# Moving SyncE's row tiles in layer one of a three-layer graph kernel

## The chip, the cores and the metric

The kernel runs on one core of a Trainium2 chip. The metric is the device time of one execution, in microseconds (us). The chip has five engines in a core that matter here: TensorE (PE in the profile, PEld for its weight loads), VectorE (DVE), ScalarE (ACT), GpSimd (POOL) and SyncE (SP), which only issues transfers.

## The reference

A graph of 6,250 nodes with 128 features each and 106,250 directed edges, sorted by their end node, each edge of one of eight types. Three layers follow one another, then a residual and a normalization of each row:

```
def layer(x, src, dst, edge_type, W, W_root, b):
    out = x @ W_root + b
    x_src = x[src]
    for r in range(8):
        mask = (edge_type == r)
        agg = segment_sum(x_src * mask, dst)
        cnt = segment_sum(mask, dst)
        out += (agg / maximum(cnt, 1)) @ W[r]
    return out
h = x
for i in range(3):
    h = layer(h, ...);  if i < 2: h = relu(h)
return layernorm(x + h)
```

## The kernel before

The edges are cut into 832 tiles of 128 edges, four tiles to a slot (`GT`), 208 slots (`NQ`) a layer. For each tile the rows `x[src]` of its 128 edges are brought from the node table in HBM to one place of `ring`, an SBUF buffer of 26 slots (`G`). Slot q lies at place q % 26 of the ring, so its tiles can only be loaded once slot q - 26 has been used.

Three engines load tiles, each in its own way:

- GpSimd loads most of them (`gather`, L432): one indirect transfer of 128 rows for each tile, L439, in order of slots. Before each slot it takes a credit `ring_free`. The instruction itself keeps GpSimd busy for about 0.94 us.
- SyncE loads 14 tiles a layer (`gather_rows`, L346), the last tile of 14 chosen slots. It reads the row numbers into registers and issues 128 transfers of one row each (L369), one tile after the other. From slot 26 on it takes a credit `sync_slot_free` ahead of a tile.
- ScalarE loads 8 tiles a layer in the same manner (`gather_rows`, L864, issued at L878), at slots 26, 50, ... 194, in pieces of 8 rows between its other work.

`owners` (L68) says which tile is whose; GpSimd leaves out what is in the list. `OWNERS[0]` is layer one's list, `OWNERS[1]` that of layers two and three: `kind` is 0 in layer one alone. Before, the two lists are equal: SyncE has slots 20, 34, 48, ... 202, 14 apart.

Each slot then passes through three engines. VectorE writes the one-hot matrices of its four tiles (`weigh`, L646). TensorE (`sum_edges`, L1135) waits for the slot's gathers, then for SyncE's or ScalarE's rows if it has such a tile, and sums the rows of each tile by node and type (L1153). ScalarE (`evacuate`, L890) gives back the slot (`ring_free`, and `sync_slot_free` if the slot 26 further on has a tile of SyncE) and copies the sums out of PSUM (L902), one copy a slot. After each second slot TensorE multiplies them by the eight weight matrices (`apply_types`, L1157), and VectorE adds the result to `out_t`.

In layer one the same three engines also look up the weight 1/count of each edge, 13 slots ahead (`turn`, `look_up`, VectorE's `cells`), so this layer has more work for each slot, up to slot 195. Ahead of it lies the setup: edges are turned to columns, counts are made, `x` is transposed. GpSimd starts to gather as soon as the source numbers are ready (`src_cols_ready`), during the setup, and SyncE too.

Between two layers TensorE turns `out_t` to rows, ScalarE and VectorE apply the relu, SyncE writes them to `node_table` in HBM, and only then gives GpSimd `table_ready`; the next layer's first gather waits for it.

Of the kernel before, what the change touches and what calls it, by code (L numbers as in the profile page):

```python
# [25 lines left out]
GT = 4  # L26
G = 26
# [8 lines left out]
NQ = NT // GT  # L36
FREES = G // 2
LOADS = 8
SYNC_TILES = 14
# [24 lines left out]
def spread(first, last, n):  # L64
    return [first + (last - first) * k // max(n - 1, 1) for k in range(n)]


def owners(kind):  # L68

    sync = {q * GT + GT - 1: "sync" for q in spread(20, NQ - 6, SYNC_TILES)}  # L70
    act = {q * GT + GT - 2: "act" for q in range(G, NQ - 8, SPACE)}
    return {**sync, **act}


OWNERS = [owners(kind) for kind in range(2)]
BPAD = BUCKETS + BWIN

# [1162 lines left out]
```

## Time and profile before

| | |
|---|---|
| median of 3 runs | 3231.51 us (3230.74 to 3236.58) |
| the profiled execution | 3242.82 us, its span 3241.0 us |
| mean granted clock of TensorE | 0.787 of full speed |
| GpSimd (POOL) busy | 2309.5 us, 71% |
| TensorE (PE) busy | 2111.5 us, 65% |
| VectorE (DVE) busy | 1251.7 us, 39% |
| ScalarE (ACT) busy | 553.7 us, 17% |

The times of the table and of all rows are microseconds from the start of the span. A share of busy time is a mean over setup, three layers and the passages between them, which differ in what they wait for; the rows below are therefore taken from single stretches. Issuing a transfer doesn't count as busy for ScalarE and SyncE, but the rows of a timeline show when transfers are issued and for how long a run of them lasts.

### The profile page before, as it was taken

To read this page: it belongs to the slowest core of one execution; us is meant where nothing else is said; L and a number is where in the kernel's file an instruction comes from. 1 tells how busy PE (TensorE), PEld (TensorE's weight loads), DVE (VectorE), ACT (ScalarE), POOL (GpSimd) and SP (SyncE) were. 2 spreads that over 40 slices of the span, in tenths; PEclk is the share of its full clock that TensorE was granted. 3 is DMA by queue.
4 is the path that set the end of the run, shared out by engine and by line. 5 is a ranking of instruction groups with operands and counts; after the bars stand their busy time and mean duration, and the time that the engine had idled before them with its cause. 6 is when DMAs were issued, how large, how long until landed. Compare 5 with 4: busy or idle time off the path is not lost. (4 is left out here: it accounts for less than half of the span.)

```text
span 3241.0 us, 78756 instructions
## 1 busy us (share of the span) xinstructions
PE 2111.5 (65%) x13004; PEld 1936.7 (60%) x13004; DVE 1251.7 (39%) x5754; ACT 553.7 (17%) x983; POOL 2309.5 (71%) x2445
## 2 busy tenths in 40 slices
PE   7977777777667566566666556556656556656656
PEld 6866666666556445555556556555555555556556
DVE  5544444444434433333333333333333333333334
ACT  1122222222222221111111111112111111111113
POOL 6657777777777177777777777747777777777773
PEclk9978888888878877777767776768777877777777
DMA  3112222222222122222222222232222222222232
GB/s 103 46 37 56 56 56 56 56 56 56 55 56 56 53 61 56 55 55 56 56 56 55 56 56 55 56 82 55 56 55 55 56 56 56 56 55 56 55 94 63
DMA packets 124472, 187.87 MB, mean 58 GB/s; under 512 B 48603, under 2 KB 82026, under 8 KB 123978
## 3 DMA queue, kind: packets, MB, share of 16 engines
q0 software_dynamic: 77760, 159.41, 18.8%
q1 hardware_dynamic: 40026, 21.85, 2.4%
q14 instruction: 375, 3.07, 0.3%
q8 instruction: 119, 1.95, 0.2%
q10 hardware_dynamic: 6192, 1.60, 0.2%
HBM read 173.06 MB, written 9.60 MB: 56 GB/s over the span
## 5 line engine op out<-in xcount | busy, mean ns | idle before, releaser
L439 POOL DMA_INDIRECT ring<-node_table,src_t x1620 | 1532.8, 946 | 586.6 <-issue 433.3
L1153 PE MATMUL ps_a<-onehot,ring 128*128 128x128 f32 x4992 | 897.0, 335 | 980.0 <-DMA ring<-node_table,src_t 755.9
L649 DVE TENSOR_SCALAR onehot<-iota,key,weight 128x128 f32<-128x128 f32 x2496 | 885.9, 368 | 1424.7 <-DVEq L266 1415.2
L1153 PEld LDWEIGHTS ps_a<-onehot,ring 128*128 128x128 f32 x4992 | 771.0, 236 | 1055.9 <-DMA ring<-node_table,src_t 710.9
L439 POOL DMA_INDIRECT ring<-in_x,src_t x810 | 774.3, 956 | 296.2 <-issue 190.1
L1163 PE MATMUL ps_o<-sums,w_rel 128*128 128x128 f32 x4992 | 937.7, 367 | 62.4 <-PEq L266 62.3
L1163 PEld LDWEIGHTS ps_o<-sums,w_rel 128*128 128x128 f32 x4992 | 917.8, 284 | 71.8 <-issue 71.8
L902 ACT COPY sums<-ps_a 128x512 f32<-128x512 f32 x624 | 364.8, 585 | 2331.4 <-ACTq L266 2174.5
L660 DVE TENSOR_TENSOR out_t<-out_t,ps_o 128x16 f32 x2496 | 437.4, 175 | 51.2 <-DVEq L266 36.4
L531 DVE TENSOR_TENSOR oh_cell<-cell_t,iota_bf 128x256 bf16<-128x256 bf16 x208 | 61.2, 295 | 407.7 <-DVEq L266 372.6
L888 ACT CAST oh_cell_t<-ps_r 64x512 bf16<-64x512 f32 x202 | 116.9, 579 | 139.9 <-ACTq L266 139.5
L1099 PE MATMUL ps_r<-ident_bf,oh_cell 128*64 128x128 bf16 x808 | 95.1, 244 | 3.1 <-PEq L266 3.0
L1099 PEld LDWEIGHTS ps_r<-ident_bf,oh_cell 128*64 128x64 bf16 x808 | 65.8, 146 | 29.0 <-issue 7.9
L1116 PE MATMUL ps_w<-inv_parts,oh_cell_t 64*128 x832 | 63.0, 169 | 14.4 <-PEq L266 13.5
L1116 PEld LDWEIGHTS ps_w<-inv_parts,oh_cell_t 64*128 64x128 bf16 x832 | 41.5, 94 | 35.6 <-issue 20.7
L1053 PE MATMUL ps_r<-h_t,w_root 128*128 128x512 f32 (+1 forms) x78 | 43.4, 682 | 27.1 <-PEq L266 25.8
L1062 PEld LDWEIGHTS ps_a<-count_bkt,count_cell 128*64 128x64 bf16 x416 | 50.9, 216 | 5.3 <-issue 5.3
L1062 PE MATMUL ps_a<-count_bkt,count_cell 128*64 128x32 bf16 x416 | 52.4, 292 | 1.1 <-PEq L266 1.1
L1062 PE MATMUL ps_o<-count_bkt,count_cell 128*64 128x32 bf16 x416 | 52.1, 291 | 0.0
L1062 PEld LDWEIGHTS ps_o<-count_bkt,count_cell 128*64 128x64 bf16 x416 | 51.2, 217 | 0.0
L1053 PEld LDWEIGHTS ps_r<-h_t,w_root 128*128 128x128 f32 x78 | 14.2, 216 | 56.2 <-issue 56.0
L578 DVE TENSOR_TENSOR count_cell<-cell_t,iota_bf 128x1024 bf16<-128x1024 bf16 x52 | 35.7, 686 | 0.0
(140 smaller groups left out, 418.0 us busy)
## 6 DMA issues: line engine op xcount, KB each, us to landing
ring<-node_table SPq DMA_DIRECT2D x3584, 0.5 KB
ring<-node_table ACTq DMA_DIRECT2D x2048, 0.5 KB
ring<-in_x SPq DMA_DIRECT2D x1792, 0.5 KB
ring<-node_table,src_t POOLq DMA_INDIRECT x1620
ring<-in_x ACTq DMA_DIRECT2D x1024, 0.5 KB
ring<-in_x,src_t POOLq DMA_INDIRECT x810
node_table<-ring SPq DMA_DIRECT2D x24, 256.0 KB
out_rows<-ring SPq DMA_DIRECT2D x12, 256.0 KB
```

What stands on the lines that cost most here:

```text
L439: nc.gpsimd.indirect_dma_start(out=ring[:, q % G, t, :], out_offset=None, in_=source, in_offset=bass.IndirectOffsetOnAxis(ap=src_t[:, q * ...
L531: nc.vector.tensor_tensor(oh_cell[:, b, :, :], cell_t[:, q * GT:(q + 1) * GT].unsqueeze(1).broadcast_to([P, CELLS, GT]), iota_bf[:, :, 0:G ...
L649: ins = nc.vector.tensor_scalar(onehot[:, b, t, :], iota_1[:, :], key[:, col:col + 1], weight[:, col:col + 1], ALU.is_equal, ALU.mult)
L660: nc.vector.tensor_tensor(here, here, ps_o[b][:, at:at + WIN], ALU.add).then_inc(added, 1)
L888: nc.scalar.copy(oh_cell_t[:, b, :], bank[0:CELLS, :]).then_inc(turned_full[b], 1)
L902: nc.scalar.copy(sums[:, b, :, at:at + GT, :].rearrange("p r t w -> p t r w"), ps_a[a][:, :].rearrange("p (t r w) -> p t r w", r=R, t=GT))\
L1053: nc.tensor.matmul(ps_r[b][:, 0:block_cols(n)], w_root[:, :], h_t[:, n * BLK:n * BLK + block_cols(n)], start=True, stop=True).then_inc(r_f ...
L1062: ins = nc.tensor.matmul(ps_c[h][0:CELLS, 0:BWIN], count_cell[:, h, :, t], count_bkt[:, h, :, t], start=(t == 0), stop=(t == CT - 1))
L1099: ins = nc.tensor.matmul(bank[0:CELLS, t * P:(t + 1) * P], oh_cell[:, b, :, t], ident_bf[:, :], start=True, stop=True)
L1116: ins = nc.tensor.matmul(ps_w[r][:, at:at + NEAR * PARTS], oh_cell_t[:, b, t * P:(t + 1) * P], inv_parts[:, bass.ds(bucket[t], NEAR), :].r ...
L1153: ins = nc.tensor.matmul(ps_a[b][:, t * KEYS:(t + 1) * KEYS], ring[:, q % G, t, :], onehot[:, b, t, :], start=True, stop=True)
L1163: ins = nc.tensor.matmul(ps_o[b][:, 0:PAIR * WIN], w_rel[:, r, :], sums[:, b, r, :, :].rearrange("p t w -> p (t w)"), start=(r == 0), stop ...
```

## The change

In layer one SyncE's 14 tiles belong to the slots 14, 24, 28, 43, 58, 74, 89, 105, 120, 136, 151, 167, 182 and 198, instead of 20, 34, 48, 62, 76, 90, 104, 118, 132, 146, 160, 174, 188 and 202. The number stays 14. The tiles of slots 20, 34, ... in layer one pass to GpSimd, those of the new slots from GpSimd to SyncE. ScalarE's tiles and layers two and three are as they were.

```
 def owners(kind):

-    sync = {q * GT + GT - 1: "sync" for q in spread(20, NQ - 6, SYNC_TILES)}
+    at = spread(20, NQ - 6, SYNC_TILES) if kind else [14, 24] + spread(G + 2, NQ - 10, SYNC_TILES - 2)
+    sync = {q * GT + GT - 1: "sync" for q in at}
     act = {q * GT + GT - 2: "act" for q in range(G, NQ - 8, SPACE)}
     return {**sync, **act}
```

## Rows read from the trace of the kernel before

**Rows 1.** The page's busy times: engine, busy us, share of the span, instructions.
```profile
PE 2111.5 (65%) x13004; PEld 1936.7 (60%) x13004; DVE 1251.7 (39%) x5754; ACT 553.7 (17%) x983; POOL 2309.5 (71%) x2445
```

**Rows 2.** Timeline of POOL: start, length, what; in brackets the idle time before.
```profile
149.06 1.37 POOL L439 DMA_INDIRECT ring<-in_x,src_t  x1 [0.30 <-issue]
188.00 0.94 POOL L439 DMA_INDIRECT ring<-in_x,src_t  x1 [37.57 <-POOLq L266]
...
1072.62 0.94 POOL L439 DMA_INDIRECT ring<-in_x,src_t  x1 [0.30 <-issue]
1137.64 0.94 POOL L439 DMA_INDIRECT ring<-node_table,src_t  x1 [64.08 <-issue]
...
2149.86 0.94 POOL L439 DMA_INDIRECT ring<-node_table,src_t  x1 [0.30 <-issue]
2179.58 0.94 POOL L439 DMA_INDIRECT ring<-node_table,src_t  x1 [28.77 <-POOLq L266]
```

**Rows 3.** Windows of L439 alone: stretch, length, POOL busy (gathers), TensorE's clock, DMA.
```profile
188.00:1074.00 886.00, 670.13 (x707) 0.84 0.21 56
1137.00:2151.00 1014.00, 766.32 (x810) 0.74 0.21 56
```

**Rows 4.** Timeline of SyncE's queue.
```profile
28.37 66.15 SPq L369 DMA_DIRECT2D ring<-in_x  x128
...
219.12 65.91 SPq L369 DMA_DIRECT2D ring<-in_x  x128
...
896.04 66.01 SPq L369 DMA_DIRECT2D ring<-in_x  x128
...
963.63 133.70 SPq L369 DMA_DIRECT2D ring<-in_x  x256
```

**Rows 5.** Who waited for L369's rows, in all layers; timeline of PE.
```profile
  PE ps_a L1153: 66.2, 7
...
692.94 2.08 PE L1153 MATMUL ps_a<-onehot,ring 128*128 128x128 f32 x8 [4.51 <-DMA ring<-in_x]
...
1098.43 2.08 PE L1153 MATMUL ps_a<-onehot,ring 128*128 128x128 f32 x8 [18.66 <-DMA ring<-in_x]
```

**Rows 6.** Windows of ScalarE's copies L902 alone, one copy a slot.
```profile
298.00:691.50 393.50, 53.69 (x92) 0.86 0.22 56
762.00:824.00 62.00, 7.73 (x14) 0.78 0.22 56
```

**Rows 7.** Timeline of ACT, L902: slots 2, 3, 26, 117, 194, 201, 203, 207; layer two's 207.
```profile
191.84 0.58 ACT L902 COPY sums<-ps_a 128x512 f32<-128x512 f32 x1 [2.28 <-ACTq L266]
...
199.93 0.58 ACT L902 COPY sums<-ps_a 128x512 f32<-128x512 f32 x1 [3.91 <-ACTq L266]
...
298.24 0.58 ACT L902 COPY sums<-ps_a 128x512 f32<-128x512 f32 x1 [1.64 <-ACTq L266]
...
691.06 0.58 ACT L902 COPY sums<-ps_a 128x512 f32<-128x512 f32 x1 [3.62 <-ACTq L266]
...
1058.93 0.58 ACT L902 COPY sums<-ps_a 128x512 f32<-128x512 f32 x1 [1.68 <-ACTq L266]
...
1080.04 0.59 ACT L902 COPY sums<-ps_a 128x512 f32<-128x512 f32 x1 [2.07 <-ACTq L266]
...
1104.44 0.58 ACT L902 COPY sums<-ps_a 128x512 f32<-128x512 f32 x1 [2.99 <-ACTq L266]
...
1114.85 0.58 ACT L902 COPY sums<-ps_a 128x512 f32<-128x512 f32 x1 [2.01 <-ACTq L266]
...
2155.69 0.58 ACT L902 COPY sums<-ps_a 128x512 f32<-128x512 f32 x1 [5.30 <-ACTq L266]
```

**Rows 8.** Windows of all engines: PE, PEld, DVE, ACT, POOL busy; clock; DMA.
```profile
298.20:416.40 118.20, 89.22 (x693) 80.69 (x692) 58.85 (x280) 30.44 (x56) 89.51 (x95) 0.88 0.22 56
...
751.70:1058.90 307.20, 206.40 (x1518) 186.12 (x1519) 133.74 (x634) 68.14 (x127) 232.13 (x247) 0.81 0.21 56
...
96.00:162.00 66.00, 64.92 (x424) 53.57 (x423) 36.99 (x75) 10.90 (x18) 41.63 (x43) 1.00 0.17 45
```

## The prediction

> **What bounds the kernel now.** I read the busy shares first, then GpSimd's gathers one by one, then what every other engine waits for in layer one. GpSimd is busy 71% of the span, more than any other engine [rows 1], and its gathers (POOL, L439) start every 1.25 us with 0.30 us between them: it is never free while a layer's gathers run. In layer one 707 gathers start between 188.00 and 1072.62, 884.62 / 706 = 1.253 us apart; layer two has 810 in one unbroken run [rows 2, 3]. Once its gathers have begun it stands still only three times: from 150.4 to 188.0, when it has filled the 26 slots of the ring and no slot has been given back; for 64.1 us between layers one and two (start to start 65.02); and for 28.8 us between two and three (29.72) [rows 2]. The same work lies between two layers both times, so 35.3 us of the first gap want a reason.
>
> The reason is SyncE. It loads its row tiles by 128 single-row transfers in 66 us, and starts one tile every 67.6 us (896.04 to 963.63) when nothing holds it [rows 4]. Its first tile (slot 20) is issued from 28.4 to 94.5; then it stands idle until 219.12, because the second tile belongs to slot 34 and slot 8 must have been used first. From there it never rests: 13 tiles end at 1097.33 (the row of 256 starts at 963.63 and takes 133.70) [rows 4], 24 us after GpSimd's last gather. TensorE waits 66.2 us for these rows in 7 waits, the first at slot 118 (4.51 us) and the last, 18.66 us, at slot 202, whose matmuls start at 1098.43, 1.1 us after the last transfer was issued [rows 5].
>
> Why it falls behind: with no wait for SyncE, the chain of TensorE, ScalarE and VectorE takes (691.06 - 298.24) / 91 = 4.317 us a slot from slot 26 to slot 117 (ScalarE's copies L902, one a slot; 92 lie in that stretch) [rows 6, 7]. 14 slots are 60.4 us against SyncE's 67.6, so each tile loses 7.2 us. The tile of slot 34 is in at 286, needed at 298.24 + 8 x 4.317 = 332.8: 46.7 us early. After 6.5 tiles that is used up, at slot 118 to 132, where the waits begin. In layer one TensorE trails GpSimd by a whole ring at first, as it starts late; in layer two it is close behind at the end: the last copy at 2155.69, the last gather at 2149.86 [rows 2, 7]. Layer one's last copy is at 1114.85, 42.2 us behind.
>
> **The change, part by part.** (1) Slots 14 and 24 both lie in the first filling of the ring, so neither waits for a free slot. SyncE issues the second right behind the first, from about 95 to 161, in time that it now idles. Slot 24 is needed near 290. Hidden; the cover is 129 us. Beside it run TensorE, busy 64.92 of 66 us [rows 8], and GpSimd, whose filling is followed by 37.6 us of standing still. That the 128 transfers slow TensorE there I can't exclude. The stretch from 28.4 to 94.5 has the same transfers with TensorE at work all the same; I take 0, with 1 us as the upper end, as they are 0.5 KB each.
>
> (2) The twelve others begin at slot 28, free after slot 2's copy at 191.84 [rows 7], instead of slot 34 at 219.12. SyncE's run starts 27 us earlier and is one tile shorter: 191.8 + 12 x 67.6 = 1003, less the last pause, plus 1.1 us for landing: in at 1002.7, 96 us before today's end.
>
> (3) Their mean distance is 170 / 11 = 15.45 slots, 66.7 us of the chain's own pace, against 67.6. So the margin hardly shrinks: slot 28 in at 259, needed at 306.9 (48 us); slot 198 in at 1003, needed at 1023.5 for slot 194, and four slots more, 1036.8 (34 us). All seven waits go. From slot 117 to 194 the copies take 1058.93 - 691.06 = 367.9 us where 77 slots at 4.317 give 332.4 [rows 7]: 35.5 us too long; and the last wait adds 18.7.
>
> (4) GpSimd gets one tile less in the ring's first filling, where it stands still afterwards, and one more behind it: 708 gathers from 188.00 instead of 707. That costs 1.25 us; the last starts at 1073.87. Between slots 29 and 33 it runs one gather earlier than today: slot 29's first could start at 200.6, and its slot is given back when slot 3's copy begins, 199.93 [rows 7]. 0.7 us of room; 0 taken, and 1.25 us the upper end. Slot 74 now has a SyncE and a ScalarE tile together, as slot 146 has before: it costs nothing, the count of gathers stays 810.
>
> (5) What is late next: without SyncE's waits the chain reaches slot 194 at 691.06 + 77 x 4.317 = 1023.5. The rest has no look-up of weights: 7 slots take 21.1 us (1058.93 to 1080.04), and the last ones 2.60 each (1104.44 to 1114.85) [rows 7], so 36.7 us for 13 slots: 1060.2. GpSimd's last gather starts at 1073.87. From about slot 200 TensorE waits for GpSimd as in layer two, and the last copy comes 5.8 us after the last gather's start, at 1079.7. Lower end: 0.94 us for the gather, 1.1 for landing as with SyncE's rows, 2.08 for the eight matmuls [rows 5], 4.1 us, 1078.0. Against 1114.85 that is 35.2 us less (up to 36.9).
>
> (6) From the last copy to the next layer's first gather it takes 22.8 us after layer one (1114.85 to 1137.64) and 23.9 after layer two [rows 2, 7]. The second ends as layer one would now end, with TensorE waiting for each slot, so I lean to it: 23.4, costing 0.6 (0 to 1.1). Layer two's first gather then starts at 1103.1, 34.6 us earlier (34.1 to 36.9; 31.8 with the 1 and 1.25 of parts 1 and 4). Layers two and three are each paced by 810 gathers and keep their lengths.
>
> Granted clock: in 298.2 to 416.4, with no wait for SyncE, TensorE's clock is 0.88 of 2.4 GHz, in 751.7 to 1058.9, with five of the waits in it, 0.81 [rows 8]. The Trainium skill (TensorE: Matmul & The Clock Gate, What's actually happening) says that the throttled state is the default and that activity releases it. By that rule the waits removed give clock back, and 4.317 us a slot or less holds to the end. The trace agrees in these two stretches, but by the rule or without it the sum is the same, as GpSimd sets the end; only rival A would lose its chance.
>
> **Sum.** Span 3241.0 - 34.6 = 3206.4, the profiled time 3242.82 - 34.6 = 3208.2. The profiled execution is 11.3 us above the median, 3231.51; nothing suggests that the difference lies in the stretches changed, so 3196.9 is the forecast.
>
> **The rivals.** A: the chain, not GpSimd, sets layer one's end, as it slows down in its second half. For: the copies behind the wait at slot 132 come 14 in 62 us, up to 4.77 us apart, at clock 0.78 [rows 6]. It decides from (1079.7 - 36.7 - 691.06) / 77 = 4.57 us a slot on. Against: 4.317 was held over 91 slots. Its worst reading: the waits up to slot 188 only covered pauses of its own, slot 194 is reached at 1058.9 as now, and the end is 1058.9 + 36.7 = 1095.6. The last wait is gone even so: 19 us, 3212. Its middle, 4.65 us a slot: 1085.8, 29 us, 3203.
>
> B: SyncE is late again. Its margins are 34 us or more, so its tile would have to take 70.4 us instead of 67.6; by the windows of rows 4 none does. If it were, with slot 198 in at 1050: 1050 + 9 x 2.6 = 1073, still before 1079.7, and nothing lost. It takes 1057 to be seen; at 1070 the end is 1094, 3211.
>
> C: no change that can be measured. It would need the last wait, 18.66 us, to be a wait for something else as well, such as ScalarE's own tile of slot 194; but slots 194 to 201 pass without one, and slot 202 holds no ScalarE tile. Also if the new list did not reach layer one; it does, as kind 0 is layer one alone. Time 3232.
>
> D, slower: TensorE at its lower level, 1.2 GHz, through the second half of layer one, now that it has no long rests. In the first stretch it is busy 89.22 us of 118.20 at 0.88, so 3.26 us of a slot's 4.317; at 0.5 that would be 3.26 x 0.88 / 0.5 = 5.7, the slot 6.8 us, and layer one ends at 691 + 77 x 6.8 + 13 slots of about 4 = 1267, 152 us later: near 3384. It costs more than it brings from (1114.85 - 36.7 - 691.06) / 77 = 5.03 us a slot. Against: no stretch shows less than 0.78 here, and the clock was higher where TensorE rested less.
>
> **How the numbers follow.** Forecast's case 0.75 (3193 to 3200), A 0.15 (3199 to 3212), B 0.03, C 0.04, D 0.03. The lower end is 36.9 us of gain and 2 us more for the spread of runs: 3192.5. The upper takes in A's middle and most of its worst: 3208. By the cases this holds 0.87; the surplus over 0.8 is for costs that I misjudge. A change of 0.2% (6.5 us) is what can be told from none. Faster 0.93 (forecast, A, B), within it 0.04, slower 0.03.
>
> **What the profile after must show.** SyncE's second tile issued at 95 to 161, the third from about 192, its last row near 1002. No wait of TensorE for SyncE's rows in layer one. GpSimd still until 188, then 708 gathers, the last starting near 1073.9. The last copy of layer one 4 to 6 us behind it, and the gap between the two layers' gathers 28 to 30 us instead of 65.0. If the copy of slot 194 comes later than 1043, A is right. If GpSimd has new pauses in layer one, parts 1 or 4 were wrong.

## The result and the profile after

The changed kernel takes 3212.36 us in the median of 4 runs (3211.51 to 3213.80), the one before 3231.12 us in the same set (3230.24 to 3236.58). The ratio is 0.9939, with a 95% interval of 0.9922 to 0.9956: 18.8 us faster, where the forecast said 34.6. The profiled execution took 3213.80 us (span 3212.0), 29.0 us less than the profiled one before (3242.82). That one is not among the executions of this set: the set's first of the kernel before took 3236.58 us, its three others 3230.24 to 3231.51.

The page's busy times, which answer to [rows 1]:

```profile
PE 2108.2 (66%) x13004; PEld 1933.1 (60%) x13004; DVE 1250.4 (39%) x5754; ACT 554.9 (17%) x983; POOL 2315.3 (72%) x2445
```

The timeline of GpSimd's gathers, as in [rows 2]; every line number is one higher now:

```profile
147.53 1.22 POOL L440 DMA_INDIRECT ring<-in_x,src_t  x1 [0.31 <-issue]
188.39 0.94 POOL L440 DMA_INDIRECT ring<-in_x,src_t  x1 [39.63 <-POOLq L267]
...
1076.84 0.95 POOL L440 DMA_INDIRECT ring<-in_x,src_t  x1 [0.30 <-issue]
1106.55 0.95 POOL L440 DMA_INDIRECT ring<-node_table,src_t  x1 [28.76 <-issue]
...
2120.77 0.94 POOL L440 DMA_INDIRECT ring<-node_table,src_t  x1 [0.30 <-issue]
2149.06 0.95 POOL L440 DMA_INDIRECT ring<-node_table,src_t  x1 [27.34 <-POOLq L267]
```

The gap between the gathers of layers one and two, start to start, was 65.02 us and is 29.71, as long as the one between two and three had been (29.72). The windows of GpSimd's gathers alone, as in [rows 3]:

```profile
188.00:1078.00 890.00, 673.51 (x708) 0.86 0.22 56
1106.00:2122.00 1016.00, 768.22 (x810) 0.73 0.21 56
```

708 gathers lie behind the filling of the ring, one more than before, as worked out. They start a little further apart than before, in the layer that was changed and in the next, which was not: (1076.84 - 188.39) / 707 = 1.2566 us in layer one (1.2530 before) and (2120.77 - 1106.55) / 809 = 1.2537 in layer two (1.2512 before).

SyncE's queue, as in [rows 4]:

```profile
28.09 66.15 SPq L370 DMA_DIRECT2D ring<-in_x  x128
...
95.72 65.81 SPq L370 DMA_DIRECT2D ring<-in_x  x128
...
192.20 65.99 SPq L370 DMA_DIRECT2D ring<-in_x  x128
...
869.47 134.24 SPq L370 DMA_DIRECT2D ring<-in_x  x256
```

The second tile follows the first at 95.7, the third starts at 192.2, and the last row is issued at 1003.7 (869.47 + 134.24) instead of 1097.3. The last two tiles follow each other without a rest: SyncE is as busy as before, only earlier. Who waited for its rows, in all three layers (66.2 us in 7 waits before [rows 5]):

```profile
  PEld ps_a L1154: 2.7, 2
  PE ps_a L1154: 1.2, 1
```

The one wait of TensorE, 1.2 us at 236.6, is put down to slot 14's rows, which had been issued by 94.2; it lies far from any end. ScalarE's copies for slots 2, 26, 117, 194 and 207, as in [rows 7]:

```profile
191.38 0.59 ACT L903 COPY sums<-ps_a 128x512 f32<-128x512 f32 x1 [1.57 <-ACTq L267]
...
289.04 0.59 ACT L903 COPY sums<-ps_a 128x512 f32<-128x512 f32 x1 [1.64 <-ACTq L267]
...
674.71 0.59 ACT L903 COPY sums<-ps_a 128x512 f32<-128x512 f32 x1 [3.62 <-ACTq L267]
...
1020.14 0.59 ACT L903 COPY sums<-ps_a 128x512 f32<-128x512 f32 x1 [2.19 <-ACTq L267]
...
1081.92 0.59 ACT L903 COPY sums<-ps_a 128x512 f32<-128x512 f32 x1 [4.13 <-ACTq L267]
```

(674.71 - 289.04) / 91 = 4.24 us a slot; slot 194 at 1020.1 (forecast 1023.5), the last copy 5.1 us behind the last gather. What TensorE waited for from 700 to 1100 us shows who paces the layer now, the gathers of GpSimd (`in_x,src_t`), no longer single rows (`in_x`), of which ScalarE's tiles are left:

```profile
PE ps_a L1154 <- DMA ring<-in_x,src_t: 51.5, 22, 4.5
PE ps_a L1154 <- PEq L267: 30.5, 25, 2.1
...
PE ps_a L1154 <- DMA ring<-in_x: 9.8, 3, 4.0
```

The windows of all engines, which answer to two of [rows 8]:

```profile
751.70:1020.00 268.30, 194.34 (x1421) 175.73 (x1421) 124.77 (x592) 64.03 (x118) 203.29 (x214) 0.83 0.21 56
96.00:162.00 66.00, 65.40 (x424) 53.71 (x423) 36.99 (x75) 10.74 (x18) 40.25 (x42) 1.00 0.17 45
```

From 751.7 us to slot 194's copy the granted clock of TensorE is 0.83 with the waits gone; it was 0.81.

So the trace does what the forecast said, nearly number by number, and the timed gain is little more than half. The experiments ask where the rest is.

### The profile page after: what moved, and what is told of

It is laid out like the page before. It is cut to its first block and busy times, and to the rows that moved or that the text cites. A ratio compares the mean times of both kernels' runs of the same rounds, so it can differ in the third digit from the quotient of the medians.

```text
span 3212.0 us, 78754 instructions
## 1 busy us (share of the span) xinstructions
PE 2108.2 (66%) x13004; PEld 1933.1 (60%) x13004; DVE 1250.4 (39%) x5754; ACT 554.9 (17%) x983; POOL 2315.3 (72%) x2445
```

## The experiments

Each set ran on one chip, with the kernel before timed beside it, and the sets fell on several chips. An execution that was profiled is called recorded here; each of these runs has one, the first of its executions. Edits are shown against the line `at = ...` in `owners` of the changed kernel, that of the 18 tiles in every layer against the kernel before; where a part of a line is shown, the rest of it stays.

**First set: both kernels again, a kernel that SyncE paces throughout, and a part of the change.**

The kernel before, no edit:

> The kernel before, unchanged, with a new profile. In question is where the 11 us went by which its profiled execution (3242.8 us) stood above its median (3231.5). Theory R (a recording makes SyncE's chain slower): the new profile shows about 3242 us again, 11 us above this run's own median, and layer one's last copy near 1115. Theory O (that one execution was an odd one, or another chip): the new profile lies within 3 us of the median near 3231, with layer one's last copy near 1104. Theory G (GpSimd's gathers are slower on this chip, 1.2537 us apart as in layers two and three after the change, not 1.2512): spacing 1.2537 in layers two and three here too, which adds 4 us to them in both kernels.

The changed kernel, no edit:

> The changed kernel, unchanged, beside the one before on one chip. All theories: median near 3212, ratio 0.992 to 0.996, profile within 2 us of the median, layer one's last gather 1076 to 1077, the gap between the gathers of layers one and two 29.7 us. If only chance set GpSimd's spacing (theory O), the last gather comes back to 1074 and the time to 3206.

Measured: the kernel before has a median of 3225.06 us (11 runs, ratio to itself 1.000, 0.9991 to 1.0009). Its recorded execution took 3237.38, the ten others 3221.19 to 3229.90. The changed kernel has 3206.42 (ratio 0.9945, 0.9931 to 0.9958), its recorded execution 3205.20, the four others 3205.11 to 3207.79. The recorded gain on this chip is 32.2 us, the timed one 18.8 (from 3225.17 us, the kernel before as timed beside the whole set). GpSimd's gathers in the two traces, first the kernel before:

```profile
188.74 0.94 POOL L439 DMA_INDIRECT ring<-in_x,src_t  x1 [37.80 <-POOLq L266]
...
1074.00 0.95 POOL L439 DMA_INDIRECT ring<-in_x,src_t  x1 [0.30 <-issue]
...
1134.82 0.94 POOL L439 DMA_INDIRECT ring<-node_table,src_t  x1 [59.87 <-issue]
...
2147.13 0.94 POOL L439 DMA_INDIRECT ring<-node_table,src_t  x1 [0.30 <-issue]
```

and the changed kernel:

```profile
187.87 0.94 POOL L440 DMA_INDIRECT ring<-in_x,src_t  x1 [39.25 <-POOLq L267]
...
1074.52 0.94 POOL L440 DMA_INDIRECT ring<-in_x,src_t  x1 [0.30 <-issue]
1102.59 0.94 POOL L440 DMA_INDIRECT ring<-node_table,src_t  x1 [27.12 <-issue]
...
2115.29 0.94 POOL L440 DMA_INDIRECT ring<-node_table,src_t  x1 [0.30 <-issue]
```

Layer two's gathers start 32.2 us earlier, the whole recorded gain. The spacing in layer one is 885.26 / 706 = 1.2539 in one and 886.65 / 707 = 1.2541 in the other, so the change doesn't slow GpSimd. Theory G, 1.2537 in layers two and three of both kernels, falls on this chip: layer two has (2147.13 - 1134.82) / 809 = 1.2513 and (2115.29 - 1102.59) / 809 = 1.2518, and the surplus is there all the same.

The pace that theory G asks for does exist. Over all the traces in which layers two and three have their 810 gathers unbroken, both layers run at 1.2508 to 1.2520 us (ten traces) or both at 1.2532 to 1.2544 (five traces: that of the result, `e7`, `e8`, `g1`, `g2`). It goes neither with the kernel, as the changed one has 1.2537 in the result and 1.2518 here, nor with the chip alone, as `e5` has 1.2514 on the chip of `e7` and `e8`. It is worth 2 us a layer.

Theory O's 3231 falls, since a recorded execution of the kernel before was 12 us above the timed ones again, and its layer one's last copy was at 1111.99, near the 1115 of theory R. On this chip the surplus belongs to the kernel before and not to the changed one. Whether it goes with the recording or with being the first execution is not told apart: in the 15 executions of the kernel before that stand beside this set, the first took 3236.67 us and the others 3220.91 to 3228.94.

18 tiles for SyncE in every layer:

```
-SYNC_TILES = 14
+SYNC_TILES = 18
```

> SyncE gets 18 tiles in each layer instead of 14, spread over slots 20 to 202, so that SyncE's chain sets the end of all three layers (17 tiles behind each other in layer one, 18 in each other). By 67.6 us a tile layer one becomes 256 us longer, the others 205 each: profile near 3898 to 3909. Theory R (0.85 us a tile slower when recorded): the median is about 45 us below the profile, 3864. Theories O and G: the median lies within 5 us of the profile.

Measured: 3921.68 us (3920.31 to 3937.42), the recorded execution 3937.42, 16.8 above the median of the three others (3920.59), and 28 us above the upper end of what was expected for it. The forecast of 45 us between recorded and timed failed. In the trace SyncE's tiles follow each other at 67.5 to 68.1 us, 67.6 in the mean of layer one, whose second to fourth tile are these:

```profile
203.53 66.20 SPq L369 DMA_DIRECT2D ring<-in_x  x128
...
271.65 65.93 SPq L369 DMA_DIRECT2D ring<-in_x  x128
...
339.16 65.93 SPq L369 DMA_DIRECT2D ring<-in_x  x128
```

So on this chip a surplus that went with each tile in all layers, 53 tiles here, is ruled out at 0.85 us a tile. 13.1 us with 13 tiles (3237.38 against 3224.3, the median of the ten others) and 16.8 with 17 leave a surplus per tile in layer one alone, or a fixed one with its scatter.

The early second tile alone:

```
-[14, 24] + spread(G + 2, NQ - 10, SYNC_TILES - 2)
+[14, 24] + spread(34, NQ - 6, SYNC_TILES - 2)
```

> Layer one's list is 14, 24 and twelve from 34 to 202: the second tile in the ring's first filling, but the third as late (from 219) and the last as late (slot 202) as before. My reasoning: SyncE's last tile is in at 1031, slot 202 needs it at 1041 at the chain's own pace, so no wait for SyncE and the same time as with the whole change, within 2 us (3212 here). The rival, that the earlier start of the third tile or the end at slot 198 carries the gain: SyncE's waits of TensorE come back at the end, 3217 or more.

Measured: 3208.20 us, ratio 0.9946 (0.9932 to 0.9960), beside 0.9945 for the whole change. TensorE waits 2.3 us for SyncE's rows in the whole trace. The tile put into SyncE's idle time carries all of the gain; the earlier third tile and the last at slot 198 add nothing that can be measured.

**Second set, on another chip.** The kernel before has 3241.45 us here (3237.00 to 3246.07).

28 tiles in layer one:

```
-at = spread(20, NQ - 6, SYNC_TILES) if kind else [14, 24] + spread(G + 2, NQ - 10, SYNC_TILES - 2)
+at = spread(20, NQ - 6, 14 if kind else 28)
```

> Layer one's list has 28 tiles for SyncE, spread over slots 20 to 202, layers two and three 14. SyncE issues 27 tiles behind each other from about 188, so layer one ends near 2030 in the recorded execution, and that takes about 4156 us. Theory R1 (when an execution is recorded, each of SyncE's tiles in layer one takes about 0.98 us longer; 13 tiles gave 12.7 and 17 gave 16.8): median 26 us below the profiled time, near 4130. Theory R2 (the recorded execution loses a fixed 12 to 13 us elsewhere in layer one, as in the start of SyncE's run): median 12 to 14 us below, near 4143.

Measured: 4162.25 us (4158.80 to 4163.15), recorded 4162.78. Neither theory's surplus is there.

18 tiles in layers two and three:

```
+at = spread(20, NQ - 6, 18) if kind else [14, 24] + spread(G + 2, NQ - 10, SYNC_TILES - 2)
```

> Layer one's list as in the change, 18 tiles in layers two and three (slots 20 to 202), where SyncE then sets both ends. Recorded: 3937.4 of the run with 18 everywhere, less 288.7 us by which the changed kernel's layer two starts earlier, 3649. If the excess of a recorded execution belongs to every tile that SyncE issues back to back (36 here): median 35 us below, near 3613. If only to layer one's tiles, as 16.8 us over all three layers with 18 tiles suggests: median within 4 us of the profile.

Measured: 3644.90 us (3643.22 to 3648.49), recorded 3645.96. No surplus, as expected for layers two and three; but as the chip shows none at all with 28 tiles in layer one, it decides nothing.

The last tile nearer, without the early second one:

```
+at = spread(20, NQ - 6, SYNC_TILES) if kind else [20] + spread(34, NQ - 10, SYNC_TILES - 1)
```

> Layer one's list is 20 and thirteen from 34 to 198: the last tile four slots nearer, but no second tile in the ring's first filling. SyncE's run still starts near 219 and ends near 1095, so slot 198 is summed at 1095 and nine slots of 2.6 us follow where five did: 10 us slower than before, 3235 on the chip of the last runs (ratio 1.003), recorded 3247. The rival, that the nearer last slot brings a part of the gain by itself: 3225 or less.

Measured: 3251.47 us, ratio 1.0031 (1.0016 to 1.0045), slower, at the forecast's 1.003. The wait for the last tile in its trace:

```profile
1095.75 2.08 PE L1154 MATMUL ps_a<-onehot,ring 128*128 128x128 f32 x8 [11.40 <-DMA ring<-in_x]
```

SyncE's chain ends when it did (its last row is issued at 1094.6), and four more slots lie behind it. The layer's last copy comes at 1122.82, 1114.85 in the first trace of the kernel before.

One tile more for SyncE:

```
-[14, 24] + spread(G + 2, NQ - 10, SYNC_TILES - 2)
+[14, 24] + spread(G + 2, NQ - 3, 13)
```

> Layer one's list is 14, 24 and thirteen from 28 to 205, 15 tiles. GpSimd issues one gather less after 188, 1.25 us; SyncE's last tile is in at 1071 in a recorded execution, slot 205 is summed at 1070 in the changed kernel. Expected: 0 to 1 us faster than the changed kernel, no difference that can be measured; if SyncE's tiles are shorter when not recorded, certainly no loss. The rival: SyncE binds again, 5 us slower or more.

Measured: 3211.07 us (3207.47 to 3214.53), ratio 0.9905 (0.9891 to 0.9919). The changed kernel was not run on this chip; its ratio in the next set is 0.9903, so no difference is seen, but the two stand on different chips. In the trace TensorE does wait for SyncE's rows again, 34.3 us in 8 waits, the last of 2.5 us at slot 205. The layer ends with GpSimd all the same: its last copy at 1081.79, 5.5 us behind the last gather at 1076.24, so these waits lie inside time that GpSimd's pace takes anyway. The trace has the slower of the two gather paces (1.2544 and 1.2536 us in layers two and three). The kernel is 30.4 us below the kernel before, not 19: the first sign that the gain is not the same in every set.

**Third set, on a third chip.** The kernel before: 3239.22 us (3235.46 to 3240.48).

> The changed kernel once more, as the fixed point of this set. It is paced by GpSimd in all layers: profile and median within 2 us of each other on every chip. If the kernel before is the one that differs from chip to chip (3225 and 3241 so far) because SyncE paces its layer one, the gain here may be anything from 18 to 30 us, and the changed kernel stays at 3206 to 3212. If GpSimd's pace differed as much, the changed kernel would move by the same amount as the one before and the gain stay at 19.

Measured: 3207.19 us (3206.91 to 3207.43), ratio 0.9903 (0.9889 to 0.9917). The gain is 32.0 us, the changed kernel within 1 us of the first set (3206.4), and only the kernel before has moved, from 3225.2 to 3239.2.

> 28 tiles of SyncE in layer one again, on another chip. Last time the median was 4162.3, 920.8 above the kernel before, 67.9 us for each of the 14 tiles more once the 30 us earlier start is added; profile and median agreed within 1 us. Theory R1 (SyncE's tiles are shorter in executions that aren't recorded, where the kernel before shows an excess of its profile of 12 us): here too the excess is twice that of the kernel before. Theory R2 (a fixed amount of layer one outside SyncE's own cadence): the excess is the same as that of the kernel before, whatever it is on this chip.

> 20 tiles of SyncE in layer one, from slot 20 to 202, the second at slot 29 (free 20 us earlier than slot 34). Six more tiles of 67.6 us less 19: 387 us above the kernel before, recorded and not, if SyncE's cadence is the same in both. By theory R1 the recorded difference stays at 387 and the timed one is up to 6 us less where the excess is large. Together with the run of 28 it gives the cadence of timed executions: (time with 28 - time with 20 - 12 us of earlier start) / 8.

The edit of the second is that of the 28 tiles with 20 in its place. Measured: 4158.07 us (4157.58 to 4158.32, recorded 4157.94) and 3631.85 (3628.22 to 3632.18, recorded 3632.13), which is 392.6 above the kernel before where 387 was expected. The formula in the expectation has a wrong sign, the earlier start is to be added: (4158.07 - 3631.85 + 12) / 8 = 67.3 us a tile in timed executions; the recorded ones give 67.2 by the same sum. The traces show 12.2 us for the earlier start (188.8 against 201.0) and a cadence of 67.6. On this chip SyncE's cadence is the same within 0.1 us, recorded or not.

> 18 tiles in layers two and three, layer one as in the change. 441 us above the changed kernel, recorded and timed, if SyncE's cadence is the same in both and differs by nothing between chips (438.5 would follow from 3644.9 on the last chip against 3206.4 on the one before it). Theory R1 for all layers: median 35 us below the profile where the kernel before has an excess of 12.

Measured: 3645.58 us (3643.55 to 3647.91), 438.4 above the changed kernel where 441 was expected; the time on the second set's chip was 3644.90.

**Three more sets.** Two kernels were to tell a shorter cadence from a fixed surplus, on a chip that shows the surplus: 28 tiles again, and 28 tiles with the second at slot 34:

```
+at = spread(20, NQ - 6, 14) if kind else [20] + spread(34, NQ - 6, 27)
```

> 28 tiles of SyncE in layer one, the second at slot 26, so that SyncE's unbroken run starts when slot 0 is used. It tells something if the kernel before has an excess of its profile over its median of 5 us or more on this chip. Theory R1 (cadence): then this one has twice that. Theory R2 (fixed, elsewhere in layer one): the same amount. Theory R3 (the time that the first eight slots take, 27.5 to 31 us in the two recorded executions of the kernel before, which moves the start of SyncE's run there and not here): no excess here. If the kernel before has no excess on this chip, none here either, and 920 us more than it.

> 28 tiles of SyncE in layer one, the second at slot 34 as in the kernel before, so that SyncE's run starts when slot 8 is used, 27 to 31 us later. Recorded 27 to 31 us above the kernel with the second at slot 26. Where the kernel before shows an excess: by R1 twice that, by R2 and R3 the same amount as the kernel before; only by R3 does it differ from the kernel with slot 26.

Measured, beside 3241.76 us (3239.12 to 3243.55) for the kernel before: 4159.37 (4154.68 to 4161.34) and 4191.53 (4185.62 to 4194.72). SyncE's unbroken run and the layer's last copy in the two traces, first with the second tile at slot 26:

```profile
188.25 66.02 SPq L370 DMA_DIRECT2D ring<-in_x  x128
...
2030.15 0.59 ACT L903 COPY sums<-ps_a 128x512 f32<-128x512 f32 x1 [2.01 <-ACTq L267]
```

and with it at slot 34:

```profile
218.73 65.94 SPq L370 DMA_DIRECT2D ring<-in_x  x128
...
2060.29 0.59 ACT L903 COPY sums<-ps_a 128x512 f32<-128x512 f32 x1 [2.01 <-ACTq L267]
```

The run starts at slot 8's release instead of slot 0's, 30.5 us later, and the layer ends 30.1 us later; the timed executions are 32.2 us apart. This chip doesn't show the surplus of the first set: the recorded executions lie 2.0 and 3.2 us above the medians.

> The kernel with 28 tiles of SyncE in layer one, the second at slot 34, on another chip. On the last one it took 4191.5, 949.8 above the kernel before, 14 tiles at 67.84. If the kernel before shows an excess of its profile over its median of 5 us or more here: by R1 (cadence) this one has twice that excess and lies 938 us or less above the kernel before; by R2 and R3 (fixed, or the start of SyncE's run) the same excess as the kernel before, and 950 above it. If there is no excess, as on the last three chips, 950 us and nothing new.

> The same kernel once more, in the hope of a chip that times the kernel before at 3225 to 3231 us with its recorded execution above that. By R1 (cadence) it is 938 us or less above the kernel before and its profile is 12 us or more above its median; by R2 and R3 it is 950 above. Otherwise 950 and nothing new.

Measured: 4189.18 us beside 3239.64 and 4185.79 beside 3238.52, 949.5 and 947.3 apart. Neither chip showed a surplus (the recorded executions are 0.2 us below and 2.1 above the medians); the last one is that of the third set. The question stayed unanswered.

## Why the prediction was wrong

The timed runs of the kernel before, by set, and what answers to them:

| set | kernel before, median us | changed kernel | gain |
|---|---|---|---|
| the result | 3231.12 | 3212.36 | 18.8 |
| first | 3225.17 | 3206.42 | 18.8 |
| second | 3241.45 | 3211.07 (15 tiles) | 30.4 |
| third | 3239.22 | 3207.19 | 32.0 |
| the three after it | 3241.76, 3239.64, 3238.52 | not run | |

- **What bounded the kernel** was right. Layer one's end hung on SyncE's run, and that on the release of slot 8: the early second tile alone brings the whole gain, the nearer last slot alone makes the kernel 0.3% slower, and a start of the run that is 30.5 us later moves the end by 30.1.
- **Parts 1 to 3** held. TensorE is as busy beside the second tile as before (65.40 of 66 us), the third tile starts at 192.2, the last row comes at 1003.7, and no wait for SyncE is left that matters, so rival B is out.
- **Part 4** held in its count. The last gather started at 1076.84 instead of 1073.87: 0.4 us by the start and 2.5 by a spacing of 1.2566 us (888.45 / 707). The first set, 1.2539 before and 1.2541 after the change, shows that the change doesn't do this. The trace of the result has the slower gather pace in its other layers too (1.2537).
- **Parts 5 and 6** held. The gap between the layers' gathers is 29.7 us where 29.2 follow from the forecast. GpSimd paces the end even sooner than at slot 200. Rival A is out: slot 194's copy came at 1020.1, not after 1043, though the result, 3212, equals the number of its worst reading. The same number came by another way. Rival D is out as well: the clock in the layer's second half rose to 0.83.
- **The recorded gain**, 29.0 us here, is the forecast's 34.6 less 3.5 us up to layer two's first gather and 2.1 us behind it. Of these 5.6 us the slower gather pace is 6.4: 2.5 in layer one and 3.9 in layers two and three, which were not changed; the other stretches differ by less than 2 us each and give 0.8 back. The prediction took both layers to keep their lengths, and no part of its range was for this. In the first set, with both traces at the same pace, the recorded gain is 32.2.
- **The step that failed** is in the sum: "The profiled execution is 11.3 us above the median, 3231.51; nothing suggests that the difference lies in the stretches changed". The sum carried the recorded execution's 34.6 us over to the timed ones in full. But the surplus goes away with the change: the changed kernel's profiled execution lies 1.4 us above its median, and the 11.7 - 1.4 = 10.3 us are what parts the timed gain of 18.8 from the recorded one of 29.0. The profiled execution before was not one of the result's set, so the clean comparison is the first set, on one chip: the recorded execution 12.3 us above the median with the kernel before, 1.2 below it with the changed one, 0.9 above it with the early second tile alone, and 15.7 above it with 18 tiles in every layer, where SyncE paces all ends. The timed executions of the kernel before had already had a part of what the change brings. The range took in 2 us for the spread of runs, and should have held the case that the surplus sits in layer one: a gain of 34.6 - 11.3 = 23.3 us, 3208.2, and with the 5.6 us by which the recorded gain fell short 3213.8.
- **What stays open**: what is shorter in those timed executions, whether it is the recording or the first place that makes the difference, and why in two of the sets and not in the other five. A cadence shorter by 0.85 us in all layers is ruled out (53 tiles, 16.8 us). A cadence shorter in layer one alone and a fixed amount of layer one both fit. That the surplus needs SyncE as the pacing engine is argued from the changed kernel, which lacks it, and not shown by a trace, as the timed executions leave none.

On the third set's chip the forecast of 34.6 us was near: 32.0 measured.

## What to carry to other kernels

A prediction from a trace is one of the recorded execution, and a second trace of the unchanged kernel, taken beside its timed runs on one chip, tells whether the two agree. Where that stands well above the median of the timed runs, ask which stretch the surplus lies in before taking it off both sides: if it may lie in the chain that the change removes, the gain shrinks by it, and the range must reach that far.

Where an engine loads at a fixed rate and falls behind, look first for a job that it can do while it would wait: here one tile moved into 124 us of idle time carried the whole gain, and the nearer last slot without it cost 10 us. A late tile of the slower loader is waited for with the work of the slots behind it still to come; compare the end of its run with the end of the main loader's.

## What the hardware showed unexpectedly

The kernel before took 3225, 3231 and 3239 to 3242 us in different sets, while the changed one stayed at 3206 to 3212. In one set the recorded execution of the first took 12.3 us more than its median, and that of the changed kernel 1.2 us less. GpSimd's gathers have two paces, 1.251 to 1.252 and 1.253 to 1.254 us, and one trace keeps one of them through layers two and three. SyncE's issue of 128 single-row transfers took 65.6 to 66.7 us in every trace, on every chip, with a pause of 1.2 to 1.9 us between tiles that follow each other (once 2.7).
